# A graph layer on one core: the test of the data moved from ahead of the main loop into it, x loaded in seven pieces, and fewer key columns

## The chip, the cores and the metric

The kernel runs on one NeuronCore of a Trainium2 chip. The metric is device time in microseconds (us) of one execution. Before the change it is 265.71 us, the median of three runs (265.67 to 265.93).

## What is computed

One layer of a graph network over N = 3125 nodes of 128 features and E = 53125 edges, whose list is sorted by destination:

```python
msg = node_feat[src] + edge_feat                                  # (53125, 128)
neigh = jax.ops.segment_sum(msg, dst, num_segments=3125)
rst = (1.0 + eps[0]) * node_feat + neigh
h = rst @ W1 + b1                                                 # 128 -> 256
h = (h - mean) * rsqrt(var + 1e-5) * gamma + beta                 # over the nodes
h = relu(h)
x = layernorm(x + h @ W2 + b2)                                    # over the features
```

## The kernel before

**Groups and windows.** The edges are cut into 208 groups of 256 (two rows of 128 partitions). Since the destinations are sorted, a group touches few neighbouring nodes: a window of 20 columns from the group's first destination. The sum over a group's edge rows is a matmul of the rows with a 0/1 matrix of 20 columns (`edge_sum`, L690), which VectorE makes by a comparison (`hits`, L920). VectorE adds each window into `aggT` at the first destination, which it holds in a register (L1022); registers are loaded 16 at a time (L1012).

**Two ways to node_feat[src].** For 50 groups GpSimd gathers the rows of x by indirect DMA and adds them to the edge rows in `egat` (L438, two gathers a group). For the other 158 the kernel counts: VectorE makes `hit_l` (low 7 bits of the source, L945) and `hit_k` (high part and place in the window, a half A of 25 x 12 = 300 columns, L949, and a half B of 25 x 16 = 400, L952, two groups at once), TensorE multiplies them into a PSUM bank (`counts_a`, L711 and L714, `counts_b`, L720), and ScalarE stores the 500 counts into the fp16 matrix `cnt` (L524). The columns of `cnt` are cut into 9 blocks of nodes, fed by 10, 12, 17, 25, 31, 31, 22, 8 and 2 groups. A block of f is complete when its last group is counted; then it is multiplied with x, in three bf16 parts of 25 tiles, so 75 matmuls (`multiply`, L682), spread over the windows in which the next block is counted. The block widths come out as 114, 180, 256, 376, 468, 466, 332, 120 and 110 columns; blocks begin to be multiplied at w = 13, 30, 52, 83, 122, 163, 192, 204, and the last one after the loop. VectorE adds each product (`add_block`, L986).

**The loop.** `for w in range(G)` runs over the 208 windows; on each engine it is unrolled, and the order is that of the program. A plan by estimated costs (`arrange`) chooses which windows are gathered ones. TensorE may run as far ahead as three PSUM banks of sums and three of counts allow; VectorE's additions lag two windows (LAG), its hits are made ahead (AHEAD, RING_K). In the first nine windows TensorE also turns x (`turn_x`, three tiles a window, L619), ScalarE scales it into `aggT` (L503), and VectorE splits it into parts (`rest`, L971, `part_3`, L979). From the 8th to the 24th counted group two matmuls with no use (L706) go along, to keep TensorE busy. At w = 14 VectorE clears the spare columns of `cnt` (L1039).

**Ahead of the loop.** The lists `dst` and `src` are loaded into 104 partitions (`dstq`, `srcq`), VectorE makes rel (place in the window, L814), hi, lo, key and carry rows (L816 to L828), TensorE turns each into 128 partitions (L582, L600), and engines copy them out of PSUM. VectorE then tests whether the data suit the main path (L837 to L858: windows no wider than 20, groups near their nominal place); TensorE spreads the answer (L605), VectorE stores it in `wide` and signals `path_known` (L872 to L874). All five engines wait for it, load it into a register and branch: the main path, or a general one that assumes nothing.

**Tail.** After the loop: last block, hidden layer in 14 pieces (L636) with its storage on ScalarE (L534) and statistics on VectorE (L1052), moments and scales, relu on both (L541 ScalarE, L1072 and L1074 VectorE), x + b2 (one GpSimd operation, L465) loaded into PSUM by matmuls with the identity (L770), second product (L781), layer norm and output.

**Loads.** SP issues `dst`, then x whole (24 tiles in one DMA, L354, and a last one of 53 rows), then slots and chunks of edges in turn; ScalarE issues `src`, small ones, the first destination of each group (`firsts`), and the weights.

## Time and profile before

| | us |
|---|---|
| median of three runs | 265.71 |
| the profiled execution | 265.49 |
| its span in the profile | 263.7 |
| TensorE (PE) busy | 240.7 (91%) |
| VectorE (DVE) busy | 187.8 (71%) |
| GpSimd (POOL) busy | 172.6 (65%) |
| ScalarE (ACT) busy | 127.9 (48%) |

The busy time of an engine is the time in which one of its instructions runs; PEld is TensorE's loading of weights, which overlaps the matmuls. "Clock" is the TensorE clock that was granted, as a share of 2.4 GHz. The chain of waits starts at the last instruction and goes back, at each step, to what released it or to the instruction before it on its engine. "issue" in it is time in which an engine waited for nothing that the profile shows, and names with a q (DVEq) are the engine's sequencer. A line such as L682 is line 682 of the kernel before.

### The profile page before, as it was taken

Reading aid. Unit: us, or ns where it says so; the run is one execution under the profiler, and the core shown is the slowest. Engines: PE = TensorE matmul, PEld = TensorE weight load, DVE = VectorE, ACT = ScalarE, POOL = GpSimd, SP = SyncE. Lnnn points to the kernel's source line nnn. Section 1 sums busy time; section 2 is a strip of 40 time slices with the busy share of each in tenths; the row PEclk is TensorE's granted clock in tenths of the full one; section 3 lists DMA queues with packets and bytes.
Section 4 is the critical chain, followed back from the end, with each engine's and each line's share of the span. In section 5 each row is a group of like instructions: output and inputs, shape, how many; then the busy total and the mean of one; then the engine's idle time right before and its main releaser. Section 6 shows DMA issues by size and latency. Waiting matters only on the chain.

```text
span 263.7 us, 6841 instructions
## 1 busy us (share of the span) xinstructions
PE 240.7 (91%) x2205; PEld 201.5 (76%) x2205; DVE 187.8 (71%) x686; ACT 127.9 (48%) x225; POOL 172.6 (65%) x113
## 2 busy tenths in 40 slices
PE   0649689999999999999999999999999999999980
PEld 0548568889999998788888888878888879845980
DVE  2978894768789986887887878777666511288882
ACT  0406512445565665455645555544444232176794
POOL 3058888888888888888888888888888600270000
PEclk9999956999999999999999999999999999999996
DMA  5975655677789888777888787877776400000034
GB/s 156 271 232 109 138 115 100 151 153 177 192 193 209 189 196 193 171 184 189 200 186 187 183 193 176 192 165 176 156 160 155 81 0 2 4 0 0 2 114 130
DMA packets 48957, 38.11 MB, mean 145 GB/s; under 512 B 5019, under 2 KB 47947, under 8 KB 48921
## 3 DMA queue, kind: packets, MB, share of 16 engines
q1 hardware_dynamic: 32829, 30.62, 40.3%
q0 software_dynamic: 14400, 6.56, 20.8%
q10 hardware_dynamic: 1692, 0.48, 1.0%
q8 instruction: 19, 0.31, 0.5%
q14 instruction: 17, 0.14, 0.2%
HBM read 36.05 MB, written 1.60 MB: 143 GB/s over the span
## 4 chain that ended last, share of the span: by engine, by line
PE 79%; DVE 12%; issue 3%; ACT 2%; DVEq 2%; DMA 1%; ACTq 1%
PE ps L682 28%; PE ps L690 20%; PE ps L720 9%; PE ps L714 7%; PE ps L636 4%; PE ps L781 3%; PE ps L706 2%; DVE hit_k L952 2%; PE ps L770 2%; DVE hit_k L949 2%; DVE aggT L1022 2%; PE ps L711 1%; ACT big L561 1%; DMA x_room<-in_dst_dram 1%; PE ps L619 1%
## 5 line engine op out<-in xcount | busy, mean ns | idle before, releaser
L438 POOL DMA_INDIRECT egat<-in_x_dram,srci x100 | 163.6, 1636 | 43.1 <-issue 28.3
L524 ACT ACTIVATE big<-ps 128x500 f32 x158 | 96.7, 612 | 109.8 <-PE ps L720 83.6
L690 PEld LDWEIGHTS ps<-hit_c,ebuf 128*128 128x128 f32 x632 | 103.2, 195 | 14.9 <-DVE hit_c L920 4.7
L690 PE MATMUL ps<-hit_c,ebuf 128*128 128x20 f32 x632 | 97.3, 232 | 6.4 <-DVE hit_c L920 4.6
L1022 DVE TENSOR_TENSOR aggT<-aggT,ps 128x20 f32 x208 | 35.9, 173 | 54.9 <-PE ps L690 35.5
L682 PE MATMUL ps<-big,xN 128*128 128x114 f16 (+8 forms) x225 | 59.7, 278 | 0.4 <-ACT big L524 0.3
L682 PE MATMUL ps<-big,x_room 128*128 128x114 f16 (+8 forms) x225 | 59.6, 278 | 0.0
L682 PE MATMUL ps<-big,xr 128*128 128x114 f16 (+8 forms) x225 | 59.5, 278 | 0.0
L720 PE MATMUL ps<-hit_k,hit_l 128*128 128x400 f16 x158 | 53.2, 337 | 0.0
L714 PE MATMUL ps<-hit_k,hit_l 128*128 128x300 f16 x158 | 46.5, 294 | 0.0
L952 DVE TENSOR_TENSOR hit_k<-iota_k,key 128x800 f16<-128x800 f16 x79 | 44.9, 568 | 0.0
L949 DVE TENSOR_TENSOR hit_k<-iota_k,key 128x600 f16<-128x600 f16 x79 | 36.6, 464 | 0.0
L690 PEld LDWEIGHTS ps<-hit_g,egat 128*128 128x128 f32 x200 | 32.7, 195 | 4.9 <-DVE aggT L1022 1.7
L945 DVE TENSOR_TENSOR hit_l<-iota_k,lo 128x512 f16<-128x512 f16 x79 | 33.2, 421 | 1.6 <-issue 1.6
L690 PE MATMUL ps<-hit_g,egat 128*128 128x20 f32 x200 | 30.5, 236 | 1.4 <-DVE aggT L1022 1.4
L682 PEld LDWEIGHTS ps<-big,xN 128*128 128x128 bf16 x225 | 25.0, 111 | 5.7 <-issue 0.9
L711 PE MATMUL ps<-hit_n,hit_l 128*128 128x25 f16 x157 | 29.3, 186 | 0.0
L720 PEld LDWEIGHTS ps<-hit_k,hit_l 128*128 128x128 f16 x158 | 28.5, 180 | 0.0
L711 PEld LDWEIGHTS ps<-hit_n,hit_l 128*128 128x128 f16 x157 | 27.1, 172 | 1.7 <-issue 0.7
L682 PEld LDWEIGHTS ps<-big,x_room 128*128 128x128 bf16 x225 | 24.2, 107 | 4.4
L682 PEld LDWEIGHTS ps<-big,xr 128*128 128x128 bf16 x225 | 24.5, 109 | 3.9
L465 POOL TENSOR_TENSOR xN<-xN,b2e 128x3200 f32<-128x3200 f32 x1 | 7.0, 6960 | 19.5 <-PE ps L682 19.5
(105 smaller groups left out, 209.3 us busy)
## 6 DMA issues: line engine op xcount, KB each, us to landing
ebuf<-in_edge_attr_dram SPq DMA_DIRECT2D x79, 256.0 KB
egat<-in_edge_attr_dram SPq DMA_DIRECT2D x49, 128.0 KB
egat<-in_x_dram,srci POOLq DMA_INDIRECT x100
out_dram<-big SPq DMA_DIRECT2D x5, 256.0 KB
w_sb<-in_L_gnn_W_dram ACTq DMA_DIRECT2D x2, 128.0 KB, 6.9
out_dram<-big SPq DMA_DIRECT2D x2, 128.0 KB
x_room<-in_dst_dram SPq DMA_DIRECT2D x1, 192.0 KB
x_room<-in_src_dram ACTq DMA_DIRECT2D x1, 192.0 KB
```

The costliest lines, as they stand in the source:

```text
L438: return nc.gpsimd.indirect_dma_start(to, None, x[:, :], bass.IndirectOffsetOnAxis(ap=ix, axis=0), compute_op=op)
L524: nc.scalar.activation(cnt[:, :, bass.ds(lows[m % LOADS], WIN)], ps[:, m % BANKS_C, 0:KEYS].rearrange("p (t n) -> p t n", n=WIN), ACT.Copy ...
L636: nc.tensor.matmul(ps[:, n % BANKS_C, 0:width(b)], w1_sb[:, h * P:(h + 1) * P], aggT[:, b * BANK:b * BANK + width(b)], start=True, stop=Tr ...
L682: last = nc.tensor.matmul(ps[:, ACC + f % 2, 0:SIZES[f]], part_v, cnt[:, t, STARTS[f]:STARTS[f] + SIZES[f]], start=(u == 0), stop=(u == UN ...
L690: last = nc.tensor.matmul(ps[:, SUMS + w % BANKS_S, 0:WIN], rows_v[:, j * D:(j + 1) * D], hits_v, start=(j == 0), stop=(j == ROWS - 1))
L711: nc.tensor.matmul(counted(m)[:, :, 0], hit_l[:, (m - 1) % RING_K, 1, :], hit_n[:, (m - 1) // CARRY % 2, (m - 1) % CARRY, :], start=True, ...
L714: nc.tensor.matmul(counted(m)[:, :, 0:WIN_A], hit_l[:, m % RING_K, 0, :], hit_k[:, m % RING_K, 0:KEYS_A].rearrange("p (t n) -> p t n", n=W ...
L720: nc.tensor.matmul(counted(m)[:, :, FROM_B:WIN], hit_l[:, m % RING_K, 1, :], hit_k[:, m % RING_K, KEYS_A:KEYS_A + KEYS_B].rearrange("p (t ...
L945: nc.vector.tensor_tensor(hit_l[:, r:r + 2, :, :].rearrange("p g j (n two) -> p (g j) n two", two=2), pairs(iota_k[:, 0:P]).unsqueeze(1).t ...
L949: nc.vector.tensor_tensor(hit_k[:, r:r + 2, 0:KEYS_A].rearrange("p g (n two) -> p g n two", two=2), pairs(iota_k[:, 0:KEYS_A]).unsqueeze(1 ...
L952: nc.vector.tensor_tensor(hit_k[:, r:r + 2, KEYS_A:KEYS_A + KEYS_B].rearrange("p g (n two) -> p g n two", two=2), pairs(iota_k[:, FROM_B:F ...
L1022: nc.vector.tensor_tensor(to, to, ps[:, SUMS + v % BANKS_S, 0:WIN], ALU.add).then_inc(window_added, 1)
```

## The change

The main path begins without the verdict, on all engines. The first destinations, which address `aggT` and `cnt`, are clamped by two VectorE operations to a range in which every access is within bounds, whatever the data. The tests are in the loop: the reductions in window 85, the rest in window 88 together with the clearing of the spare columns (before in window 14), the matmul that spreads the answer after window 91, its storage and `path_known` in window 94. Each engine branches late: SP after all loads, GpSimd after x + b2, ScalarE and VectorE before the hidden layer's storage and statistics, TensorE after the first four of the preloads of x + b2. If the verdict is bad, the general path loads the lists and x again and does all over.

In the head, key rows are made before lo, PSUM copies of rel, sources and carry go from VectorE to ScalarE, the matmul that shares b2 stands behind four turns, and the row buffers lie in the last columns of `cnt`, since the first ones are now written early. x is loaded in seven pieces, each with a semaphore, between chunks and slots; the weights move from ScalarE's queue to the end of SP's.

Half B of the keys has 15 columns a tile instead of 16 (375 instead of 400; VectorE makes 376 for two to be handled at once), against a list of numbers of its own that starts at 5. MARGIN, the allowed distance from the nominal place, is 30 instead of 36. There are 8 blocks instead of 9; by the same arithmetic their widths are 120, 180, 256, 376, 468, 466, 332 and 218, begun at w = 14, 30, 52, 83, 123, 163, 193 and after the loop. The diff, cut to its core:

```diff
-FROM_B = 4
-WIN_B = WIN - FROM_B
+FROM_B = 5
+WIN_B = 15
-BLOCKS_C = (10, 12, 17, 25, 31, 31, 22, 8, 2)
+BLOCKS_C = (10, 12, 17, 25, 31, 31, 22, 10)
-MARGIN = 36
+MARGIN = 30
+        TEST_F = 3
+        W_BOUNDS = READY[TEST_F] + 2
+        W_TESTS = W_BOUNDS + 3
+        W_WORST = W_TESTS + 3
+        W_SHARED = W_WORST + 3
...
 SP:
-            sp.dma_start(xN[:, 0:NT - 1, :], x_main).then_inc(x_loaded, 16)
-            for n in range(SLOTS):
+            chunk(0)
+            x_piece(X_ORDER[0])
+            slot(0)
+            x_piece(X_ORDER[1])
+            chunk(1)
...
+            for n in range(3, SLOTS):
                 slot(n)
-                if n < CHUNKS:
-                    chunk(n)
+            sp.dma_start(w1_sb[:, :], w1).then_inc(weights_loaded, 16)
...
 GpSimd, ahead of the gathers:
-            pool.wait_ge(path_known, 1)
-            flag = pool.value_load(wide[0:1, 0:1], min_val=0, max_val=1)
+            pool.wait_ge(sources_made, 1)
...
 ScalarE:
+            act.wait_ge(rel_turned, 1)
+            nc.scalar.activation(spread(rel[:, :]), banked(2), ACT.Copy).then_inc(rel_made, 1)
...
+            act.wait_ge(src_turned, 1)
+            nc.scalar.activation(spread(srci[:, :]), banked(7)[:, QC:Q, :], ACT.Copy).then_inc(sources_made, 1)
+            act.wait_ge(carry_turned, 1)
+            nc.scalar.activation(carry[:, :].rearrange("p (q h) -> p q h", h=2),
+                                 ps[:, 1, 0:GC].rearrange("p (h q) -> p q h", q=QC), ACT.Copy).then_inc(carry_made, 1)
...
             act.wait_ge(path_known, 1)
             flag = act.value_load(wide[0:1, 0:1], min_val=0, max_val=1)
+            with act.If(flag == 0):
+                store(hidden_made, hidden_stored)
+            with act.Else():
...
 TensorE:
+                if w == W_WORST:
+                    pe.wait_ge(worst_found, 2)
+                    pe.wait_ge(block_added, TEST_F)
+                    nc.tensor.matmul(ps[:, ACC + (TEST_F + 1) % 2, 0:1], ones[0:Q, :], over[:, TESTS + 1:TESTS + 2],
+                                     start=True, stop=True).then_inc(worst_shared, 1)
...
+            pe.wait_ge(x_b2_added, 1)
+            preload(0, 4)
             pe.wait_ge(path_known, 1)
             flag = pe.value_load(wide[0:1, 0:1], min_val=0, max_val=1)
+            with pe.If(flag == 0):
+                pe.wait_ge(hidden_stored, NB * HH)
+                preload(4, len(ROW_PIECES))
+                products()
+            with pe.Else():
...
 VectorE, ahead of the loop:
+            dve.wait_ge(rel_made, 1)
+            hits_c(0)
             dve.wait_ge(firsts_loaded, 32)
+            dve.wait_ge(constants_made, 10)
+            nc.vector.tensor_tensor(firsts[:, :], firsts[:, :], least_first[:, 0:G], ALU.max).then_inc(lows_made, 1)
+            dve.wait_ge(lows_made, 1)
+            nc.vector.tensor_tensor(firsts[:, :], firsts[:, :], most_first[:, 0:G], ALU.min).then_inc(lows_made, 1)
...
 VectorE, in the loop:
-                    if w == SPREAD * NB:
-                        nc.vector.memset(cnt[:, :, CNT - SPARE:CNT], 0.0).then_inc(spare_zeroed, 1)
+                if w == W_BOUNDS:
+                    find_bounds()
+                if w == W_TESTS:
+                    find_worst()
...
+                    nc.vector.memset(cnt[:, :, CNT - SPARE:CNT], 0.0).then_inc(spare_zeroed, 1)
+                if w == W_SHARED:
+                    dve.wait_ge(worst_shared, 1)
+                    nc.vector.tensor_scalar(wide[:, :], ps[:, ACC + (TEST_F + 1) % 2, 0:1], 0.5, None,
+                                            ALU.is_gt).then_inc(wide_made, 1)
+                    dve.wait_ge(wide_made, 1)
+                    nc.vector.memset(tick[:, 0:1], 0.0).then_inc(path_known, 1)
```

## Rows read from the trace of the kernel before

**Rows 1.** the page: clock and traffic in 40 slices; chain by engine; gathers.

```profile
PEclk9999956999999999999999999999999999999996
...
GB/s 156 271 232 109 138 115 100 151 153 177 192 193 209 189 196 193 171 184 189 200 186 187 183 193 176 192 165 176 156 160 155 81 0 2 4 0 0 2 114 130
...
PE 79%; DVE 12%; issue 3%; ACT 2%; DVEq 2%; DMA 1%; ACTq 1%
...
L438 POOL DMA_INDIRECT egat<-in_x_dram,srci x100 | 163.6, 1636 | 43.1 <-issue 28.3
```

**Rows 2.** chain of waits, head; columns: start us, us, what.

```profile
5.57 0.69 DVE big L814
...
9.17 0.59 DVE most L837
...
11.48 0.15 DVE over L858
11.63 0.50 DVE rel L868
...
12.60 0.89 DVE key L879 x2
...
13.73 0.56 DVEq L886
...
14.71 0.54 issue
...
15.32 0.34 DVE hit_l L945
...
16.90 0.61 PE ps L690 x2
```

**Rows 3.** timeline of the head; columns: start us, us, engine, line, operation.

```profile
6.03 0.76 PE L577 MATMUL ps<-row,ones 1*128 1x129 f32 x2 [6.03 <-DMA row<-in_L_gnn_eps_dram]
...
6.72 1.66 PE L582 MATMUL ps<-ident,big 104*128 104x104 f32 x8
...
15.62 1.69 POOL L438 DMA_INDIRECT egat<-in_x_dram,srci  x1 [12.99 <-DMA egat<-in_edge_attr_dram]
```

**Rows 4.** windows; columns: length, each engine's busy us, clock, DMA share, GB/s.

```profile
29.00:32.00 3.00, 1.57 (x14) 1.15 (x12) 2.15 (x5) 1.68 (x3) 2.39 (x2) 1.00 0.66 116
38.00:44.00 6.00, 6.00 (x37) 4.79 (x36) 3.99 (x13) 1.22 (x2) 5.08 (x4) 0.50 0.49 94
104.00:108.00 4.00, 3.29 (x29) 2.25 (x27) 2.87 (x10) 1.87 (x4) 3.39 (x3) 1.00 0.89 200
108.00:116.00 8.00, 8.00 (x81) 6.88 (x80) 6.97 (x26) 4.58 (x8) 6.78 (x5) 1.00 0.72 164
```

**Rows 5.** chain of waits, middle of the loop.

```profile
87.72 0.09 DVE hit_k L949
...
106.69 0.40 PE ps L690 x2
```

**Rows 6.** groups by line and shape, 30 to 225 us.

```profile
L720 PE MATMUL ps<-hit_k,hit_l 128*128 128x400 f16 x151 | 50.2, 333 | 0.0
L714 PE MATMUL ps<-hit_k,hit_l 128*128 128x300 f16 x151 | 43.9, 290 | 0.0
L952 DVE TENSOR_TENSOR hit_k<-iota_k,key 128x800 f16<-128x800 f16 x73 | 41.5, 568 | 0.0
```

**Rows 7.** chain of waits, last windows and tail.

```profile
221.58 1.00 PE ps L682 x19
...
224.83 3.65 PE ps L682 x75
...
244.82 9.14 PE ps L781 x80
```

**Rows 8.** timeline of VectorE: the clearing; the ready second half of block 0.

```profile
40.62 0.81 DVE L1039 MEMSET big<- 128x900 uint32 x1
...
242.84 0.43 DVE L1074 TENSOR_SCALAR big<-big 128x512 f32<-128x512 f32 x1
```

More of the change, by code:

```diff
@@ L574, in _ @@
             pe.wait_ge(ident_made, 1)
-            pe.wait_ge(row_loaded, 32)
-            pe.wait_ge(constants_made, 2)
-            nc.tensor.matmul(ps[:, 7, 0:D + 1], ones[0:1, :], row[0:1, :], start=True, stop=True).then_inc(b2_shared, 1)
             def turn(bank, v, n):
@@ L621, in turn_x, with hidden @@
                         last.then_inc(x_turned, 1)
+            def hidden(n0, n1, complete, made, stored):
+                for n in range(n0, n1):
+                    b, h = n // HH, n % HH
+                    pe.wait_ge(complete, b + 1)
+                    if n >= BANKS_C:
+                        pe.wait_ge(stored, n - BANKS_C + 1)
+                    nc.tensor.matmul(ps[:, n % BANKS_C, 0:width(b)], w1_sb[:, h * P:(h + 1) * P],
+                                     aggT[:, b * BANK:b * BANK + width(b)], start=True,
+                                     stop=True).then_inc(made, 1)
@@ new lines, in _, with preload @@
+            multiply(F - 1, 0, UNITS)
+            pe.wait_ge(counts_stored, GC)
+            pe.wait_ge(weights_loaded, 80)
+            hidden(0, NB * HH, sums_complete, hidden_made, hidden_stored)
+            def preload(a0, a1):
+                for a in range(a0, a1):
+                    t0, t1 = ROW_PIECES[a]
+                    r = rows_of(t1 - 1)
+                    nc.tensor.matmul(ps[0:r, (a + 4) % 8, 0:(t1 - t0) * D], ident[0:r, 0:r],
+                                     xN[0:r, t0:t1, :].rearrange("p t d -> p (t d)"), start=True, stop=False,
+                                     skip_group_check=True)
@@ L773, in _ @@
[L773 to L783 removed]
+                pe.wait_ge(gen_sums_complete, NB)
@@ L824, in _ @@
                                            in1=rel_h[:, :, P:GROUP], op0=ALU.mult, op1=ALU.add).then_inc(key_rows_made, 1)
+            nc.vector.scalar_tensor_tensor(out=loq, in0=hiq, scalar=float(-P), in1=srcq, op0=ALU.mult,
+                                           op1=ALU.add).then_inc(place_rows_made, 1)
+            dve.wait_ge(key_turned, 1)
+            key_d = key[:, :, :].rearrange("p (q k) two -> p q k two", k=HJ)
+            for a in range(2):
+                last = nc.vector.tensor_copy(key_d[:, :, :, a], banked(3)[:, 0:QC, :])
+            last.then_inc(key_made, 1)
             nc.vector.tensor_tensor(eq_h, dst_h[0:QC, :, P:GROUP], next_h[0:QC, :, :].to_broadcast([QC, 2, P]),
@@ L876, in _ @@
-            dve.wait_ge(key_turned, 1)
-            key_d = key[:, :, :].rearrange("p (q k) two -> p q k two", k=HJ)
-            for a in range(2):
-                last = nc.vector.tensor_copy(key_d[:, :, :, a], banked(3)[:, 0:QC, :])
-            last.then_inc(slots_made, 1)
-            dve.wait_ge(carry_turned, 1)
-            nc.vector.tensor_copy(carry[:, :].rearrange("p (q h) -> p q h", h=2),
-                                  ps[:, 5, 0:GC].rearrange("p (h q) -> p q h", q=QC)).then_inc(slots_made, 1)
```

818 lines of the change are left out of this document (436 added, 382 removed).

## The prediction

> **What bounds the kernel now.** I read the page first, then the chain of waits in order of time, then windows and the timeline where the chain changed engine. TensorE holds 79% of the chain, VectorE 12% [rows 1]. But a share over the whole says little here, because there are three kinds of stretch.
>
> The head: up to 16.90 us TensorE has no window to work on. The chain is VectorE's alone [rows 2]: from the landing of the destination list (5.57) through place and key rows, the minima and maxima, the tests (to 11.63), the copies out of PSUM, the load of the verdict (13.73) and the jump behind it, to the first key hits at 15.32. Then, to about w=12, VectorE remains the later engine: TensorE waits on its additions, and TensorE's clock is granted at 0.50 (the 1.2 GHz level) for about 10 us around 38 to 44 [rows 1, 4].
>
> The loop from there: the chain lies on TensorE, except 87.72 to 106.69, where it is VectorE's without a break [rows 5]. By the code's plan block 2 ends before w=83 and is added at w=84; in the chain that addition comes some three microseconds before the stretch ends, so the stretch ends at about w=86.
>
> The tail, from 224.83: last block, hidden layer, preloads, second product, all on TensorE [rows 7].
>
> **The head, step by step.** VectorE's work between 9.17 and 12.60 is mostly tests and copies. What goes: minimum, maximum and tests, 9.17 to 11.63 = 2.46 us; the copies of rel and srci and the verdict, 11.63 to 12.60 = 0.97, less 0.05 for the padding that stays; the copy of carry, 0.24 (from 12.60 + 0.89 to 13.73); verdict load and jump, 13.73 to 15.32 = 1.59. Sum 5.22 us [rows 2]. What comes: two operations on the 208 first rows, not in the trace; bounds 0.3 (two small tests at 0.15 each, the 11.48 row) and 1.2 (two of 0.59, the reduction of 512 elements at 9.17); I take 0.6, nearer the small ones since one partition of 208 elements is under half of 512, plus two waits. And two waits on TensorE's turns. From the list's landing at 5.57, a 0.69 and four operations of about 0.4 make the key rows, which no longer wait for lo: ready near 7.4. Turning rel and key takes 4 transposes each, half of the 8 in 1.66 us [rows 3], so key is turned at about 8.3, where VectorE arrives at 8.0: 0.3 us. The shared bias now stands behind four turns (rel, key, lo, src, to 9.9 us) and takes 0.76 [rows 3]; VectorE, at 10.0 with carry, waits for it until about 10.6: 0.6. ScalarE takes over the copies; it has 5 fewer DMAs to issue before them, and its copy of lo ends near 10, srci and carry near 11, before VectorE asks. So VectorE gains 5.2 - 0.6 - 0.9 = 3.7; less 0.2 for waits not counted, **3.5 us** (2.5 to 4.5). The first key hits then start at about 11.9, and TensorE's first counts about 13.2. Since to w=12 VectorE is the later engine and its work there is otherwise unchanged, the whole shift is kept. GpSimd moves too: its first gather stood behind the verdict, at 15.62 [rows 3], and may start near 10.5. Its 100 gathers take 1.64 us and 0.30 of issue each [rows 1], 194 us in all: before, done near 210 where the last window ends at 224.8; now near 205 against some 218. It stays some 13 us ahead.
>
> **Seven pieces of x.** Costed at nothing: chunk 0 and x piece 0 are first on SP's queue, 0.5 MB; behind them the pieces alternate with chunks and slots. If traffic moves as before (156 GB/s in the first 6.6 us, 0.4 MB of it lists, then 271 [rows 1]), the first two are there near 6.5 us, piece 4 near 8, chunk 1 near 9, the last piece of x near 16; that one is turned from w=8 (over 20 us) and split from w=7. The cover is thick for x, thinner for the first rows (`firsts`), which VectorE now needs near 11.3 instead of 13.73 [rows 2]: the trace shows only that they had landed by then. Bounds 0 and 2.4 us; I take 0, since nothing waited. The weights, moved behind the slots on SP, are used 200 us later.
>
> **Keys of 375 columns.** Counts of half B: the 400-column matmul is 333 ns, the 300-column one 290 [rows 6], 0.43 ns a column, so 25 columns are 10.8 ns. Of 158 groups some 137 lie where TensorE is on the chain: 1.5 us. In VectorE's stretches its own hits shrink from 800 to 752 elements, 6% of 568 ns = 34 ns per pair of groups [rows 6], some 10 pairs, 0.3. Together **1.8 us** (0 if the odd stride of 15 costs what the columns save; 2.1 if all groups count). The 34 filler matmuls lose 25 columns too: 21 ns at half clock, 10 at full, **0.4 us**.
>
> **Blocks.** Sizes from the code: the last three were 332, 120, 110 columns, now 332 and 218. In the loop 75 matmuls of 120 columns go: 19 take 1.00 us, so 3.95 us; at the end 75 of 110 took 3.65 [rows 7], and 218 columns at 2.4 GHz are 91 ns plus the 3 ns seen at 110 (48.7 against 45.8), 7.05 us: 3.4 more. Net **0.55 us** gained; bounds 0 and 1.
>
> **The tests in the loop.** Now at w=85 (minimum, maximum: 2 of 0.59 = 1.18 [rows 2]), w=88 (the rest of the 2.46, 1.28, and the clearing of the spare columns, 0.81 [rows 8], which before lay at w=14, while TensorE was busy throughout [rows 4]), w=94 (0.2): together 3.5 us on VectorE. They come at the very end of the stretch in which VectorE was last (to 106.69 [rows 5]), and from 108 to 116 it is busy 6.97 of 8 us [rows 4]. Queued behind them are its own additions and key hits; TensorE may run only some two windows ahead of the additions. The slack in ten windows is about 1 us. So **2.4 us** of it is paid (bounds 0.8, if the ring of hits covers each piece, and 3.5, if none is covered). TensorE's one-column product lies where it waits anyway; bounds 0 and 0.76, the first row of [rows 3], and I put 0.1. The verdict is out near w=96, its first wait is at w=123: no wait.
>
> **The tail.** Each engine now branches there. GpSimd, SyncE: off the chain. ScalarE and VectorE jump over the general path between last statistics and moments; a jump was followed by 0.54 us without work [rows 2]. Block 0 of the second relu half was ready at 242.84 + 0.43 = 243.27 [rows 8], TensorE came to it at 244.82 [rows 7]: 1.5 us of cover, so 0; without it 0.54. TensorE loads the verdict between its preloads. VectorE's whole load and jump was 1.59 us [rows 2]. Before TensorE's stand four preloads of 512 columns, over 2 us on the array, so if its sequencer works ahead of the array it is hidden. Bounds 0 and 1.6; I take 0.2 for both. The Trainium skill, "Runtime: NRT & Kernel Launch", section "Instruction fetch mechanics", says that a taken branch to a page not held forces a fetch before work goes on; no row shows such a fetch apart from the 0.54 us; by that row nothing is added behind the 1.5 us of cover, by a longer fetch only what exceeds it. "TensorE: Matmul & The Clock Gate" (its table of specifications) gives TensorE a queue of 64, by which the second branch would be hidden whole.
>
> **Sum.** -3.5 -1.8 -0.4 -0.55 +2.4 +0.1 +0.2 = -3.55 us. The profiled execution took 265.49 us (span 263.7, 1.8 around it); less 3.55 is 261.9, and against the median of the runs, 265.71, **262.2 us**.
>
> **The rivals.**
> A: the stretch at half clock is shorter or falls away, since all before it moves. It came after TensorE had been starved near 30 us (busy 1.57 of 3). From 38 to 44 TensorE was busy 6.00 of 6 at half, 3.0 of work at 2.4 GHz; VectorE wanted 3.99 less the clearing's 0.81 [rows 4, 8], with its gaps about 3.5. So 2.5 us would go there and 0.4 beside it: 259.3. For it: filler matmuls meet an earlier start. Against: the starving itself is unchanged.
> B, the slower one: the tests starve TensorE near w=85 to 95 as the head did near 30 us, and the clock falls there. Price: 3.5 instead of 2.4, and 10 us at half as in [rows 1], up to 5 us lost, less 1 where VectorE leads: 262.2 + 1 + 4 = 267.2. It decides if TensorE starves there as it did between 29 and 32 us, before the clock fell. Against: 104 to 108 had 3.29 of 4 busy without a fall [rows 4].
> C: the tests are hidden (0.8 paid): 260.6.
> D: the head is bound by transfers, and starting sooner only waits for `firsts` or chunks: the 3.5 are gone, 265.7. Against: nothing in the trace waits on those loads, which are now first in the queue.
>
> **Chances.** Forecast 0.62 (own range 260.3 to 264.3), A 0.14, C 0.08, D 0.07, B 0.09. A difference of 0.2% (0.53 us) is about what can be told from none: faster 0.84, same 0.07, slower 0.09. The range takes in A's and D's times, each widened by what the bounds of head and tests add: 258.5 to 266.2; B is left out, with little else.
>
> **What would show it.** Key hits starting at 11 to 12.5 us (head); counts matmuls of half B near 322 ns (keys); 75 final matmuls in about 7 us; TensorE waits on VectorE's additions of about 2.4 us near w=85 to 95; hidden layer to second product as long as before. Wrong if counts start after 14 us, if granted clock 0.50 appears after 100 us, or if the half-clock stretch changes by over 4 us.

## The result, and the profile after

The changed kernel took 269.62 us, the median of four runs (267.22 to 271.2), against 265.69 for the kernel before (265.31 to 265.93): 1.0142 times as long, 95% interval 1.0084 to 1.0199. The prediction was 262.2 with a range of 258.5 to 266.2, and faster at 0.84. It was slower. Twelve more runs later gave 267.18 (265.16 to 271.17), ratio 1.0048, interval 1.0015 to 1.0080; the sixteen together have a median of 268.0. So the sign stands, and the size is 1.5 to 4 us. The intervals leave out executions more than 1.5% above the fastest of their kernel (four of these twelve, six of the ten in e10), which is why there the ratio doesn't match the medians. The experiments ran on three chips; the median of the kernel before was 265.62 to 266.15 us beside them, and each ratio is against the executions on the same chip.

The page of the changed kernel's profiled execution (271.2 us, the longest of the sixteen; span 269.3), which stands against [rows 1]: TensorE's busy time; the granted clock in 40 slices; the shares of the chain.

```profile
PE 248.5 (92%) x2130; PEld 207.6 (77%) x2130; DVE 185.8 (69%) x684; ACT 128.6 (48%) x228; POOL 176.5 (66%) x116
...
PEclk9999958999999999579999999999999999999996
...
PE 80%; DVE 10%; issue 2%; ACT 2%; DMA 2%; DVEq 2%; ACTq 1%
```

TensorE's share of the chain rose from 79 to 80% and VectorE's fell from 12 to 10%, and the kernel still got longer. The clock row says where to look. Its first fall, at slices 6 and 7, is that of [rows 1]. The second, at slices 17 and 18 (108 to 121 us), is new.

The head, from the timeline (start us, length us, engine, line, operation; in brackets what ended the idle time before it), against [rows 2, 3]:

```profile
6.86 0.69 DVE L930 TENSOR_TENSOR big<-big 104x512 f32<-104x512 int32 x1 [4.99 <-DMA big<-in_dst_dram]
...
9.73 0.91 DVE L944 CAST key<-ps 128x316 f16<-128x316 f32 x2 [0.45 <-PE ps L661]
...
11.84 0.29 DVE L952 COPY b2e<-ps 128x129 f32<-128x129 f32 x1 [0.45 <-PE ps L679]
...
12.38 1.76 POOL L510 DMA_INDIRECT egat<-in_x_dram,srci  x1 [8.80 <-ACT srci L569]
12.49 0.36 DVE L1062 TENSOR_TENSOR firsts<-firsts,big 1x208 int32<-1x208 int32 x1
...
13.25 0.41 DVE L1014 TENSOR_TENSOR hit_l<-iota_k,lo 128x512 f16<-128x512 f16 x1
...
14.55 0.43 PE L769 MATMUL ps<-hit_k,hit_l 128*128 128x300 f16 x1 [1.02 <-DVE hit_k L1021]
```

The first key hits start at 13.25 us; before they started at 15.32. That is 2.1 us earlier, not the 3.4 of the forecast. The first row shows why: the destination list lands at 6.86, before at 5.57. From the landing to the first key hits it is 6.39 us, and 9.75 before, a gain of 3.4 us, so the working from one to the other was right. The two clamps are 0.36 each (I had 0.3 for one), and each wait on TensorE's turns 0.45 (I had 0.3 and 0.6). GpSimd's first gather starts at 12.38, where 10.5 was forecast; nothing waits for it.

The middle, from the chain in order of time, against [rows 5]:

```profile
101.60 0.41 DVE aggT L1055
...
102.05 1.10 DVEq L1082
...
103.36 0.18 DVE aggT L1100
...
103.79 0.46 DVE hit_k L1018
104.25 0.46 DVE hit_k L1021
104.72 0.28 DVE hit_n L1032
104.99 0.60 DVE most L959
105.59 0.59 DVE least L960
...
106.32 0.40 PE ps L739 x2
```

At w = 85 everything comes together: the addition of block 2 (L1055), the loading of 16 registers (L1082, 1.10), key hits (L1018, L1021), carry hits (L1032), and now the two reductions. Between the window additions at 103.36 and at 106.18 there is none, and TensorE, which may run only some two windows ahead, mostly stands still. The windows of that stretch (busy us of PE, PEld, DVE, ACT and POOL with instruction counts, then granted clock, DMA share, GB/s), against [rows 4]:

```profile
104.00:106.00 2.00, 0.46 (x4) 0.21 (x3) 2.00 (x5) 0.15 (x1) 1.70 (x2) 1.00 0.87 196
106.00:108.00 2.00, 1.68 (x16) 1.42 (x17) 1.57 (x7) 0.60 (x1) 1.70 (x2) 0.97 0.46 80
108.00:110.00 2.00, 2.00 (x11) 1.56 (x10) 1.59 (x14) 0.65 (x1) 1.70 (x2) 0.50 0.85 163
...
116.00:118.00 2.00, 2.00 (x12) 1.66 (x13) 1.05 (x4) 0.63 (x2) 1.54 (x1) 0.50 0.75 164
118.00:120.00 2.00, 2.00 (x20) 1.72 (x20) 1.16 (x5) 0.98 (x2) 1.73 (x1) 0.97 0.46 82
```

From 104 to 106 us TensorE is busy 0.46 of 2. Then its clock is granted at 0.50, the 1.2 GHz level, for 10 us: 11 matmuls run from 108 to 110 us, where 20 do from 118 to 120 (the counts in brackets). This is rival B, which had 0.09.

The end, from the longest pieces of the chain, against [rows 7]:

```profile
226.69 7.01 PE ps L731 x75
...
244.43 5.57 PE ps L833 x16
250.00 9.14 PE ps L847 x80
```

The last 75 matmuls take 7.01 us (forecast 7.05). From the start of the second product to the end it is 19.3 us, 18.9 before: 0.4 more, where 0.2 was forecast for the branches. That the branches cause it was not tried.

### The profile page after: what moved, and what is told of

Read it like the earlier page. It is cut to its first block, busy times and chain, and to the rows that moved or that the text cites. A ratio compares the mean times of both kernels' runs of the same rounds, so it can differ in the third digit from the quotient of the medians.

```text
span 269.3 us, 6711 instructions
## 1 busy us (share of the span) xinstructions
PE 248.5 (92%) x2130; PEld 207.6 (77%) x2130; DVE 185.8 (69%) x684; ACT 128.6 (48%) x228; POOL 176.5 (66%) x116
## 4 chain that ended last, share of the span: by engine, by line
PE 80%; DVE 10%; issue 2%; ACT 2%; DMA 2%; DVEq 2%; ACTq 1%
PE ps L731 28%; PE ps L739 20%; PE ps L775 10%; PE ps L769 7%; PE ps L711 4%; PE ps L847 3%; PE ps L761 2%; PE ps L833 2%; DVE hit_k L1021 2%; DMA big<-in_dst_dram 2%; PE ps L766 2%; DVE hit_k L1018 1%; ACT big L643 1%; DVE xr L1040 1%; DVE aggT L1100 1%
## 5 line engine op out<-in xcount | busy, mean ns | idle before, releaser
L510 POOL DMA_INDIRECT egat<-in_x_dram,srci x100 | 166.5, 1665 | 40.3 <-issue 28.0
L739 PEld LDWEIGHTS ps<-hit_c,ebuf 128*128 128x128 f32 x632 | 107.6, 202 | 12.1 <-DVE aggT L1100 4.0
L739 PE MATMUL ps<-hit_c,ebuf 128*128 128x20 f32 x632 | 99.5, 236 | 3.2 <-DVE aggT L1100 2.5
L731 PE MATMUL ps<-big,xr 128*128 128x120 f16 (+7 forms) x200 | 59.3, 298 | 0.0
L731 PE MATMUL ps<-big,x_room 128*128 128x120 f16 (+7 forms) x200 | 59.3, 298 | 0.0
L731 PE MATMUL ps<-big,xN 128*128 128x120 f16 (+7 forms) x200 | 59.2, 298 | 0.1
L775 PE MATMUL ps<-hit_k,hit_l 128*128 128x375 f16 x158 | 56.2, 356 | 0.0
L1021 DVE TENSOR_TENSOR hit_k<-iota_b,key 128x752 f16<-128x752 f16 x79 | 42.8, 542 | 0.0
L1018 DVE TENSOR_TENSOR hit_k<-iota_k,key 128x600 f16<-128x600 f16 x79 | 36.6, 463 | 0.0
L731 PEld LDWEIGHTS ps<-big,xN 128*128 128x128 bf16 x200 | 22.5, 112 | 5.3 <-issue 0.4
L731 PEld LDWEIGHTS ps<-big,xr 128*128 128x128 bf16 x200 | 22.6, 113 | 4.4 <-issue 0.5
```

The source lines that it names most:

```text
L510: return nc.gpsimd.indirect_dma_start(to, None, x[:, :], bass.IndirectOffsetOnAxis(ap=ix, axis=0), compute_op=op)
L731: last = nc.tensor.matmul(ps[:, ACC + f % 2, 0:SIZES[f]], part_v, cnt[:, t, STARTS[f]:STARTS[f] + SIZES[f]], start=(u == 0), stop=(u == UN ...
L739: last = nc.tensor.matmul(ps[:, SUMS + w % BANKS_S, 0:WIN], rows_v[:, j * D:(j + 1) * D], hits_v, start=(j == 0), stop=(j == ROWS - 1))
L775: nc.tensor.matmul(counted(m)[:, :, FROM_B:WIN], hit_l[:, m % RING_K, 1, :], hit_k[:, m % RING_K, KEYS_A:KEYS_A + KEYS_B].rearrange("p (t ...
L1018: nc.vector.tensor_tensor(hit_k[:, r:r + 2, 0:KEYS_A].rearrange("p g (n two) -> p g n two", two=2), pairs(iota_k[:, 0:KEYS_A]).unsqueeze(1 ...
L1021: nc.vector.tensor_tensor(hit_k[:, r:r + 2, KEYS_A:KEYS_A + KEYS_E].rearrange("p g (n two) -> p g n two", two=2), pairs(iota_b[:, :]).unsq ...
```

## Where the time lies, kernel by kernel

The same milestones were read from the timeline and chain of every kernel: the start of the addition of block 0 (the end of the head), of block 2 and of block 3 (the tests lie between), and of the last 75 matmuls.

| kernel | block 0 | 2 | 3 | 2 to 3 | last 75 | block 0 to last 75 |
|---|---|---|---|---|---|---|
| before | 59.04 | 103.06 | 137.51 | 34.45 | 224.83 | 165.79 |
| changed | 57.28 | 101.60 | 143.18 | 41.58 | 226.69 | 169.41 |
| changed, again (e14) | 58.24 | 102.57 | 140.75 | 38.18 | 224.23 | 165.99 |
| no tests (e2) | 57.06 | 101.40 | 136.89 | 35.49 | 220.36 | 163.30 |
| tests spread (e13) | 58.09 | 102.42 | 139.25 | 36.83 | 222.70 | 164.61 |
| before + tests' work (e3) | 59.99 | 103.82 | 140.61 | 36.79 | 227.93 | 167.94 |
| before + 375 keys (e4) | 59.08 | 103.31 | 137.86 | 34.55 | 225.81 | 166.73 |
| before + 350 keys (e9) | 58.15 | 101.28 | 135.06 | 33.78 | 221.20 | 163.05 |
| no tests, 350 keys (e7) | 53.58 | 96.90 | 131.59 | 34.69 | 213.25 | 159.67 |

One profile a kernel, so differences under a microsecond are not to be trusted: the changed kernel and e14 are the same program, and block 0 differs by 0.96. But the column "2 to 3" says what the tests cost in the loop: against the kernel without them 1.3 us spread, 2.7 with the clock at half for some 3.4 us, 6.1 with it at half for 10 us.

## Experiments

**e1: the tests earlier.** The same tests in windows 32 to 41, one block edge after the first.

```diff
-        TEST_F = 3
+        TEST_F = 1
```

> The changed kernel with its tests in the stretch of block 1 (windows 32 to 41) instead of block 3 (85 to 94); nothing else. Theory S (starving): in the profile of the changed kernel the additions of blocks 2 and 3 are 41.6 us apart against 34.4 before, VectorE's tests leave TensorE busy only 0.46 of 2 us near 105, and the clock then stands at 0.50 from 108 to 118. So the tests' place costs some 7 us, and here, where VectorE was busy 1.2 to 2.2 of 3 us, most of it returns: 262 to 264. Rival K (the keys or blocks): the loss lies in the odd stride of 15 columns or in the new blocks and not in the tests: 268 to 270.

Measured: 269.49 us (267.88 to 271.82, 4 runs), ratio 1.0183 (1.0105 to 1.0261). Theory S missed. The time is what rival K named, but the trace shows that this place is no better: TensorE starves there too (busy 2.44 of 4 us from 60 to 64 us), the granted clock is 0.77 and 0.80 in the two windows of 4 us behind it, and block 0 to block 1 takes 23.2 us instead of the 19.2 of the changed kernel.

**e2: no tests.** All minima, maxima and comparisons left out; the verdict is set to good by a constant; the clearing stays at w = 88.

```diff
-                nc.vector.tensor_reduce(most[:, :], rel_t, AX_X, ALU.max)...
-                nc.vector.tensor_reduce(least[:, :], rel_t, AX_X, ALU.min)...
...
+                nc.vector.memset(over[:, TESTS + 1:TESTS + 2], 0.0).then_inc(worst_found, 2)
```

> The changed kernel without the tests' work: the minima, maxima and comparisons are left out, the verdict is set to good by one clearing of a column; the clearing of the spare columns stays in window 88, and so do all waits and branches. Theory S: no fall of the clock after 100 us, 261 to 263, at most 1.5 us from the kernel with early tests. Rival K: 268 to 270. Rival L (the clearing alone is enough to bring the clock down): 266 to 269, with a stretch at 0.50 after 105 us.

Measured: 265.01 us (263.57 to 267.45, 10 runs), ratio 0.9984 (0.9943 to 1.0025), between what theory S and rival K named; no half clock after 100 us. Windows of its trace, as above:

```profile
104.00:106.00 2.00, 1.32 (x13) 0.94 (x13) 1.57 (x8) 0.08 (x1) 1.70 (x2) 1.00 0.94 218
106.00:108.00 2.00, 2.00 (x20) 1.50 (x19) 1.86 (x6) 1.42 (x3) 1.69 (x2) 1.00 0.57 138
```

Two things follow. The tests cost the changed kernel 2.2 us in the medians (267.18, on another chip) and 4.6 against its first four runs. And without any test the rest of the change gains 0.4 us by the ratio and 1.1 by the medians, where the forecast had 6.05 (3.55 + 2.4 + 0.1): most of the miss has nothing to do with the tests.

**e3: the kernel before, with the tests' work added in the loop.** Same sizes of VectorE operations at w = 85 and 88, on other data and with no use for the result; the clearing moved from w = 14 to 88. The tests ahead of the loop stay.

```diff
+                    if w == READY[3] + 2:
+                        nc.vector.tensor_reduce(most[:, :], again, AX_X, ALU.max)...
+                        nc.vector.tensor_reduce(least[:, :], again, AX_X, ALU.min)...
+                    if w == READY[3] + 5:
+                        for k in range(10): nc.vector.tensor_scalar(over[:, 2*k:2*k+2], spot, ...)
+                        ...
-                    if w == SPREAD * NB:
                         nc.vector.memset(cnt[:, :, CNT - SPARE:CNT], 0.0)
```

> The kernel before, its head untouched, with VectorE work of the size of the tests added in windows 85 (two reductions of 104 x 512 values) and 88 (twelve small operations), and the clearing of the spare columns moved from window 14 to 88. Theory S: the clock falls after 100 us here too, and the time grows by 5 to 8 us to 271 to 274. Rival K: the tests' work is worth at most its own 3.3 us, below 269.

Measured: 269.2 us (268.3 to 269.77, 4 runs), ratio 1.0146 (1.0082 to 1.021). Theory S missed: the profile has no half clock after 100 us, although TensorE is busy only 1.00 of 2 us from 106 to 108. The interval from block 2 to 3 is 2.3 us longer, which is the forecast's 2.4. The time is 3.05 us longer than the 266.15 measured beside it; about 0.95 of that lies ahead of block 0 in the profile, before the added work. So the work's own price was sized rightly here, and it lengthens the kernel without any fall of the clock; in e13 the same work, spread, costs 1.3, so the 2.3 is no fixed price.

**e4: the kernel before, with 375 keys** and the margin of 30.

```diff
-FROM_B = 4
-WIN_B = WIN - FROM_B
+FROM_B = 5
+WIN_B = 15
-MARGIN = 36
+MARGIN = 30
```

> The kernel before with 375 columns of keys in half B, and with the allowed distance from the nominal place at 30 instead of 36, which makes room for the second list of numbers (block widths 120, 180, 256, 376, 468, 466, 332, 120 and 98). Theory S: this part gives about what was forecast, 1.8 us and 0.4 for the fillers: 263.2 to 264.2. Rival K: 266 or more.

Measured: 266.44 us (264.3 to 267.56, 10 runs), ratio 1.0032 (0.9996 to 1.0069). Missed: no gain at all, although the margin alone shortens the last block from 110 to 98 columns (its 75 matmuls 3.26 us instead of 3.65). Groups of matmuls from 120 to 175 us, where the clock is at 2.4 GHz (line, engine, output and inputs, shape, count, busy us, mean ns of one), first e4, then e5:

```profile
L724 PE MATMUL ps<-hit_k,hit_l 128*128 128x375 f16 x48 | 16.3, 339 | 0.0
...
L686 PE MATMUL ps<-big,x_room 128*128 128x468 f16 x25 | 9.1, 363 | 0.0
```

```profile
L720 PE MATMUL ps<-hit_k,hit_l 128*128 128x400 f16 x49 | 16.1, 329 | 0.0
L714 PE MATMUL ps<-hit_k,hit_l 128*128 128x300 f16 x49 | 14.1, 288 | 0.0
...
L682 PE MATMUL ps<-big,x_room 128*128 128x468 f16 x25 | 9.0, 359 | 0.0
```

**e5: the margin of 30 alone** on the kernel before.

```diff
-MARGIN = 36
+MARGIN = 30
```

> The kernel before with the allowed distance at 30 instead of 36 and nothing else: the row of cnt is 2416 instead of 2422 columns long and the blocks begin at 120, 300, 556, 932 instead of 114, 294, 550, 926. Theory P (pitch): in the keys kernel and in the one without tests the block matmuls of 468 columns took 362 ns against 359 and those of 376 columns 324 against 321, though their widths are unchanged; if the new pitch of cnt does that, it is 362 and 324 here too, and with some 600 such matmuls the time grows by about 0.5 to 1.5 us. Rival: it came with the keys: 359 and 321 here, time unchanged within 0.3 us.

Measured: 266.0 us (265.17 to 269.88, 10 runs), ratio 1.0026 (0.9988 to 1.0065): no difference that can be told. The 375-column count takes 339 ns, the 400-column one 329: fewer columns take longer. The block matmuls, unchanged, take 3 to 4 ns more (363 against 359) in the kernel with 375 keys and not in the one with the margin alone, so that comes with the keys as well.

**e6: 375 keys from an even column.** The kernel without tests, half B at columns 4 to 18; the last column of each window is left out of the counts, so the output lacks those edges, and two more filler matmuls go along in each of the first three groups. One run.

```diff
-FROM_B = 5
+FROM_B = 4
-                nc.tensor.matmul(counted(m)[:, :, FROM_B:WIN], ...
+                nc.tensor.matmul(counted(m)[:, :, FROM_B:FROM_B + WIN_B], ...
```

> The changed kernel without the tests' work, half B written to columns 4 to 18 of each tile instead of 5 to 19 (15 columns still, an even start), so edges in column 19 are left out of the counts; two more fillers in each of the first three groups set the column that is then never written, and the fillers' weights are 0/1 values. The 375-column matmul of half B took 339 ns against 329 for 400 columns and 318 expected. If the odd start costs it, about 318 here; if the odd number of columns does, about 328; if the stride of 15 in the moving data does, 339.

```profile
L779 PE MATMUL ps<-hit_k,hit_l 128*128 128x375 f16 x49 | 16.2, 330 | 0.0
```

At full clock 300 columns take 288 ns and 400 take 329 (e5), 0.41 ns a column, which makes 319 for 375. e4 lies 20 ns above that line and e6, at 330, 11: 9 ns go with the odd start, 11 stay with the odd width of 15: none of the three values expected. The keys are read in the same way in both kernels, so the start can only matter on the output's side, in the PSUM bank; for the width this was not separated. The one run took 264.71 us, which is e2's time within what a single run tells.

**e7: 350 keys**, half B at columns 6 to 19, 14 wide, on the kernel without tests. The main path then suits fewer lists: in half B no edge may lie ahead of column 6 of its window. One run.

```diff
-FROM_B = 5
-WIN_B = 15
+FROM_B = 6
+WIN_B = 14
```

> The changed kernel without the tests' work, with half B on columns 6 to 19 (14 a tile, 350 in all), so edges of half B in column 5 are left out of the counts. By the slope of 0.43 ns a column below the 329 ns of 400 columns it is 308 ns; if a cost of some 20 ns comes with the odd start and number only, it is 308; if it comes with any other stride than 16, 328.

Measured: 257.81 us (the kernel before beside it 265.62), and 308 ns a count, as expected and on the line (288 + 50 x 0.41), and the block matmuls are back at 359. It is 7.2 us less than e2. In the table 3.6 of these lie between block 0 and the last 75 (some 140 counts x 31 ns = 4.3, less where VectorE sets the pace), and 3.5 in the head, which is another matter (below).

**e8: tests in the first block, 400 keys**, on the changed kernel (windows 16 to 25; the wait of the one-column product on the block's addition goes, since no block is added yet).

```diff
-        TEST_F = 3
+        TEST_F = 0
-FROM_B = 5
-WIN_B = 15
+FROM_B = 4
+WIN_B = 16
```

> The changed kernel with the tests in windows 16 to 25, where TensorE ran at half clock and VectorE was busy 0.18 of 3 us (41 to 44 us), and with 400 columns of keys again. Theory S: the tests cost under 1 us there and the clock stands at 1.00 from 45 us on: against the kernel without tests (265.0) the keys give back about 1: 263.5 to 265. Rival: TensorE is starved by any 3 us of VectorE work in the loop wherever it stands: 267 to 269.

Measured: 264.46 us (263.33 to 265.46, 10 runs), ratio 0.9982 (0.9952 to 1.0012). As expected. Better than the changed kernel by 2.7 in the medians, 1.8 by the ratios, and no fall of the clock after 45 us; but the edit changes place and keys at once, and what each gives was not separated.

**e9: the kernel before with 350 keys.** The edit of e4 with 6 and 14.

> The kernel before with half B of the keys at columns 6 to 19 instead of 4 to 19: 14 columns, 350 keys (and the margin of 30); nothing else. Theory W (the price of a count matmul follows its columns as long as the width per tile is even; the 15 columns of the changed kernel fall off that line): 308 ns instead of 329 for the second half, 158 windows x 21 ns = 3.3 us, so 262 to 262.8. Rival (the counts' matmuls end earlier but TensorE then waits for the key hits of VectorE, as long as before): 265 to 266.

```profile
L724 PE MATMUL ps<-hit_k,hit_l 128*128 128x350 f16 x49 | 15.1, 308 | 0.0
...
L686 PE MATMUL ps<-big,x_room 128*128 128x468 f16 x25 | 9.0, 358 | 0.0
```

Measured: 261.93 us (261.19 to 264.42, 10 runs), ratio 0.9893 (0.9852 to 0.9934). Theory W holds: 21 ns less a count, 3.9 us less in all, 0.4 of it from the shorter last block that comes with the margin. Two columns a tile taken away instead of one give more than the 2.2 us that I had booked for one.

**e10: the changed kernel with 350 keys**, the edit of e7, tests at w = 85.

> The changed kernel with 350 keys instead of 375, tests at their place in window 85. Theory W: 31 ns less in each of 158 counts (339 to 308) and 3 ns less in the four block matmuls of a window, 4.9 + 1.9 = 6.8 us: 262 to 263.5. If the width of 15 is only dear in some positions, and the 7 us between the two kernels without tests came from other places of the half clock: 265 to 268.

Measured: 266.21 us, ratio 0.9895 (0.9848 to 0.9942). The ten runs lie in two groups: four from 261.81 to 264.68, six from 266.11 to 267.71. The profiled one (267.38) is of the upper group:

```profile
104.00:108.00 4.00, 2.62 (x26) 2.29 (x27) 3.47 (x18) 1.25 (x2) 3.28 (x3) 1.00 0.68 100
108.00:112.00 4.00, 2.59 (x22) 2.15 (x20) 3.29 (x17) 1.18 (x2) 3.39 (x3) 0.90 0.63 135
112.00:116.00 4.00, 4.00 (x24) 3.39 (x25) 3.10 (x13) 1.18 (x2) 3.39 (x3) 0.50 0.73 138
```

TensorE is busy 2.62 and 2.59 of 4 us while the tests run, and then the clock is at 0.50. The lower group is about where theory W put it (262 to 263.5). The mean granted clock on record is 0.978 to 0.980 in all six of the upper group, as in the traced one, and 0.958 or 0.987 in the lower four. That the lower group is without the fall is not shown: none of the four has a trace, and the kernel before, which has no tests in the loop, splits too (beside e1 fifteen executions up to 266.55 us and four from 267.72 to 269.55).

**e11: tests in the first block and 350 keys** (the edits of e8 and e7).

> The changed kernel with 350 keys and the tests in windows 16 to 25 (first block). With 400 keys and the tests there it took 264.5; 21 ns x 158 = 3.3 us less gives 261.1, and the same difference as between the kernels without tests (375 to 350: 7 us) would give 258 to 259. Above 262: the tests there cost more once TensorE needs less time per window.

Measured: 262.18 us (260.75 to 263.01, 6 runs), ratio 0.986 (0.9816 to 0.9904): 2.3 less than e8 (3.2 by the ratios, the two ran on different chips), where 3.3 was expected. No fall of the clock after the head, and no second group in six runs.

**e12: the dst list ahead of the large loads**, on the changed kernel.

```diff
+            sp.wait_ge(dst_loaded, 80)
             chunk(0)
             x_piece(X_ORDER[0])
```

> The changed kernel (375 keys, tests in window 85), with SyncE waiting for the dst list to land before it issues the first chunk of edges and the first piece of x. Theory H (the list lands 1.3 us later than before because these loads share the DMA engines with it): the list is there at 5.6 us instead of 6.9, the first key hits 1.3 us earlier, and the time 1.0 to 1.3 us shorter, 268.3. Rival (what then comes late is the first chunk and x, issued 3.4 us later, and the first windows wait for those): 269.5 to 271. If the list lands at 6.9 all the same, the loads were not the cause.

Timeline of its head:

```profile
5.81 0.69 DVE L931 TENSOR_TENSOR big<-big 104x512 f32<-104x512 int32 x1 [3.95 <-DMA big<-in_dst_dram]
...
12.19 0.41 DVE L1015 TENSOR_TENSOR hit_l<-iota_k,lo 128x512 f16<-128x512 f16 x1
```

The list is there at 5.81 instead of 6.86, and the first key hits start at 12.19 instead of 13.25: the loads issued behind the list were what held it up. The size varies: the ten traced kernels with the changed kernel's loads have the list at 6.20 (e14) to 7.35 us, the three that wait for it at 5.54 to 5.81. I had costed the seven pieces of x at nothing by asking whether they would be there in time, and not what they would do to the 0.2 MB that stand ahead of them. The time, 266.44 us (265.53 to 270.35, 10 runs), ratio 1.0037 (0.9993 to 1.0081), is 0.7 below the changed kernel's twelve runs, within what the two measurements can tell. The profile, which has the clock at 0.54 and 0.61 from 108 to 112 us, says why so little came of it: see the next section.

**e13: the tests spread.** One reduction in window 86, one in 88, the comparisons in 89 to 92, the clearing in 94, the one-column product in 95.

```diff
-                if w == W_BOUNDS:
-                    find_bounds()
-                if w == W_TESTS:
-                    find_worst()
+                if w == W_BOUNDS + 1:
+                    find_bounds(False)
+                if w == W_BOUNDS + 3:
+                    find_bounds(True)
+                if W_TESTS <= w <= W_TESTS + 3:
+                    find_worst(w - W_TESTS)
```

> The changed kernel with the same tests cut into single steps: one reduction in window 86, one in 88, the comparisons in 89 to 92, the clearing in 94, the one-column product in 95. VectorE does the same work, but never more than some 0.7 us of it between two windows. If the starving of TensorE and the fall of the clock behind it are the larger part (rival B): no half clock after 100 us, and the time near that without tests plus what is left of the work, 265 to 266.5. If the tests' work itself costs it, wherever it stands: 269 to 270, as the changed kernel.

**e14: the changed kernel once more**, unedited, on the same chip.

> The changed kernel once more, unedited, beside the spread one. If the fall of the clock is the larger part, its times lie in two groups, one near 267 without the fall and one near 270 to 271 with it. If the tests' work is all of it, the times lie together near 269.6.

Measured: e13 266.58 us (264.41 to 268.65, 12 runs), ratio 1.0031 (0.9991 to 1.0071); e14 267.18, as above. Windows of e13, then of e14:

```profile
104.00:106.00 2.00, 1.32 (x10) 0.74 (x8) 1.80 (x7) 0.71 (x2) 1.70 (x2) 1.00 0.71 167
106.00:108.00 2.00, 2.00 (x20) 1.73 (x21) 1.80 (x6) 0.71 (x2) 1.70 (x2) 1.00 0.60 123
...
110.00:112.00 2.00, 1.43 (x14) 1.07 (x13) 1.81 (x15) 0.45 (x1) 1.70 (x2) 1.00 0.75 182
112.00:114.00 2.00, 2.00 (x21) 1.70 (x19) 1.86 (x7) 1.18 (x3) 1.70 (x2) 1.00 0.84 183
```

```profile
104.00:106.00 2.00, 1.42 (x10) 0.71 (x7) 1.67 (x6) 0.79 (x2) 1.70 (x2) 1.00 0.78 166
106.00:108.00 2.00, 0.72 (x8) 0.65 (x9) 1.57 (x6) 0.00 (x0) 1.70 (x2) 1.00 0.47 98
108.00:110.00 2.00, 2.00 (x14) 1.60 (x13) 1.90 (x14) 0.97 (x2) 1.70 (x2) 0.61 0.69 149
110.00:112.00 2.00, 2.00 (x13) 1.35 (x12) 1.68 (x10) 0.87 (x2) 1.70 (x2) 0.54 0.41 59
112.00:114.00 2.00, 2.00 (x23) 1.86 (x23) 1.60 (x8) 0.59 (x1) 1.70 (x2) 1.00 0.76 176
```

Spread, TensorE never falls under 1.32 of 2 us and keeps its full clock; in one piece it is busy 0.72 of 2 and the clock falls for some 3 us. All four traced executions with the tests in one piece at w = 85 (the changed kernel, e10, e12, e14) show such a fall. How much starving it takes these traces don't tell: e3, busy 3.88 us of the 6 from 106 to 112, kept its clock, and e10, busy 5.21 of 8, lost it.

The twelve times of e14 lie eight from 265.16 to 268.6 and four from 269.53 to 271.17, less cleanly apart than I had expected. The mean granted clock, on record for each execution, tells a little more. Of the changed kernel's sixteen, five have 0.984 or 0.985, as e14's traced one with its fall, and take 268.6 to 270.06 us; three have 0.992 or 0.993, as e13's traced one without, and take 266.21 to 267.22. So the fall seems not to be in every execution; it is an inference, since two of the sixteen have a trace. Spreading is worth 0.6 us in the medians and 1.45 in the means (266.53 against 267.98), which is twice the standard error of 0.7. What it leaves is the work: e13 is 1.6 above e2 in the median, 1.25 by the ratios.

**e15: 350 keys, tests in the first block, dst list first** (e11 + e12).

> 350 keys, tests in windows 16 to 25, and SyncE waiting for the dst list before its first chunk. With 350 keys and the tests there it took 262.2; the list 1.05 us earlier should give 261.1. If TensorE leaves half speed in the head earlier as well, as in the 257.8 kernel: 258 to 259.

**e16: 350 keys, tests spread, dst list first** (e13 + e7 + e12).

> 350 keys, the dst list first, and the tests spread over windows 86 to 95. From the changed kernel: keys -6, list -1.05, no fall of the clock -3.5, which gives 259 to 260 from 269.6. If the tests' own work is the larger part: 262 to 263.

Measured: e15 259.84 us (259.35 to 260.8, 6 runs), ratio 0.9808 (0.9765 to 0.9851); e16 260.36 (257.44 to 262.76, 6 runs), ratio 0.9786 (0.9716 to 0.9857). Both beat both kernels, by 2% or so; e15's runs lie closer together. e15 lies between its two expected values, e16's median just above its first. e15 is 2.3 below e11, 1.4 by the ratios. The earlier list is the only edit between them, but in e11's trace TensorE is at half speed without a break until 43.10 us and in e15's it isn't, so how much the list gives by itself stays open.

## The head: TensorE at half speed where the granted clock says 1.00

The 300-column count matmul is a gauge of TensorE's speed. In the changed kernel's timeline:

```profile
24.64 0.43 PE L769 MATMUL ps<-hit_k,hit_l 128*128 128x300 f16 x1
...
27.88 0.29 PE L769 MATMUL ps<-hit_k,hit_l 128*128 128x300 f16 x1
...
34.19 0.43 PE L769 MATMUL ps<-hit_k,hit_l 128*128 128x300 f16 x1
...
43.44 0.29 PE L769 MATMUL ps<-hit_k,hit_l 128*128 128x300 f16 x1
```

0.43 us up to 24.64, 0.29 from 27.88, 0.43 again from 34.19 to 41.57, 0.29 from 43.44. Only the second slow stretch shows as a granted clock of 0.50; in the first the windows say 1.00 and the matmuls take as long as at 0.50. The Trainium skill, "TensorE: Matmul & The Clock Gate", Part 1, says that half rate is the state from which the engine starts, and that activity lifts it; it also warns that the recorded clock events are not reliable. The trace agrees with the start at half rate and with the warning. It does not bear out the rise by activity as simply as that: in e12 TensorE is busy 27.76 of the 28 us from 14 to 42 and still at 0.43 at 42.47. In the kernel before the first slow stretch ends between 23.35 and 24.50 and the second lies from 35.10 to 41.85.

The end of this half speed, more than the start of the key hits, sets where the head ends. In e12, e13 and e14 the matmul is at 0.43 without a break until about 42 us; from e12:

```profile
42.47 0.43 PE L770 MATMUL ps<-hit_k,hit_l 128*128 128x300 f16 x1
...
44.05 0.29 PE L770 MATMUL ps<-hit_k,hit_l 128*128 128x300 f16 x1
```

Block 0 is added at 57.90, 58.09 and 58.24, later than in the changed kernel (57.28), although their key hits start at 12.19, 12.87 and 12.59 instead of 13.25. In the traces of all kernels but e16, block 0 is added 13.2 to 15.7 us after the first 300-column matmul that is back at 0.29 for good, whether the key hits started at 11.9 or at 15.6. In e7 TensorE is at full speed from 20.26, slow again by 28.43 and fast from 37.87 on: block 0 at 53.58. In e16 it stays fast from here on:

```profile
29.62 0.42 PE L770 MATMUL ps<-hit_k,hit_l 128*128 128x300 f16 x1
...
31.28 0.29 PE L770 MATMUL ps<-hit_k,hit_l 128*128 128x300 f16 x1
```

and block 0 is added at 52.71, 5.4 us earlier than in e13 with the same work but for the keys and the list. So a head of nearly the same code differs by some 5 us with when TensorE comes up to speed. What decides that in one kernel and not in the next I can't say; no run was made for it alone.

## Why the prediction was wrong

By the terms of its sum:

- **Keys, -1.8 and -0.4: wrong.** e4 gives +0.85 by its ratio (-0.1 to 1.8), so 2.2 to 3 us of the miss, the margin's possible share included. The step that failed is "25 columns are 10.8 ns": the slope between two even widths was applied to an odd one. I had written the case down as a bound ("0 if the odd stride of 15 costs what the columns save") and then taken the other end, with no row for it. It wasn't even the end: 339 against 329 lies beyond it.
- **Head, -3.5: mis-sized, and one step wrong.** The first key hits came 2.1 earlier (2.7 in e14), block 0's addition 1.8 (0.8 in e14). The operations were right to 0.15 us; missing was the later landing of the list, 1.3 us (0.6 in e14), which e12 traced to the loads behind it. The step that failed besides is "the whole shift is kept", since VectorE was to stay the later engine up to w=12. From 14 to 42 us TensorE is busy 22.29 of 28 before and 27.77 in e14, nearly all of it at half speed, and its waits on VectorE's additions there shrink from 2.5 us to 0.2: what comes earlier runs into TensorE itself.
- **Tests in the loop, +2.4: right for the work** (2.3 in e3; 1.3 when spread), but in the changed kernel a fall of the clock came on top, 3.8 us in the profiled execution (6.1 against 2.3) and 0.4 to 1.4 in e14's (2.7 against 2.3 or 1.3).
- **Rival B, 0.09: too small.** It was priced at 267.2 and decided by "if TensorE starves there as it did between 29 and 32 us", and it did: 0.46 of 2. What I held against it, that 104 to 108 had 3.29 of 4 busy, was the kernel before without the tests in that place. The two reductions of 1.2 us, behind a register load and three hit operations in the same window, had to be laid over those rows and weren't. Moreover the range left B out whole.
- **Blocks, -0.55: near its lower bound of 0,** as far as one profile each can tell: 7.01 at the end against 7.05; in the loop e2 and e4, which share the 375 keys and the margin, differ by 3.43 us between block 0 and the last 75, against 3.95. That leaves a gain of 0.1 (3.43 less the 3.36 by which 7.01 exceeds 3.65).
- **Tail, +0.2:** 0.4 to 0.8 in all kernels with the late branch, cause not tried. The four preloads ahead of TensorE's load, put at "over 2 us", take some 1.4 us by the 16 in 5.57 above. **One-column product, +0.1:** TensorE waits there for nothing that the chain shows.

Added up from the profiles of the kernel before and of e2, whose profiled executions differ by 0.5 us where 6.05 was forecast without the tests: the head 1.5 short (3.5 against 2.0), the keys 3.1 (0.94 lost in e4 between block 0 and the last 75, 2.2 forecast), the blocks 0.5, the tail 0.5. Together 5.6, where 5.55 is to be explained; the sum has to agree, since the terms divide one difference, but how they divide it rests on one profile a kernel. The tests are no part of the miss in the twelve runs: 2.2 us against the 2.5 forecast. In the first four runs they cost 4.6, so there 2.1 us more of the miss are theirs.

## What to carry to other kernels

Before a matmul's width is cut, look whether the new width and start per tile are even: here runs of 14 cost 21 ns less than runs of 16, and runs of 15 from an odd column 10 ns more. Work moved into a loop that has slack on average should be cut to the size of the slack between two steps and kept away from windows in which loads of registers and other batches fall; the sum of busy time in ten windows says nothing on whether the other engine starves for two microseconds, and for TensorE that can be followed by microseconds at half its clock. A load that is wanted first should be finished, not only issued first, before megabytes are put behind it: that brought the list 0.4 to 1.8 us forward, though in e12 nothing that can be told from noise in the time. And before an earlier start is booked as gained, look at what the engine that takes over does with it: here TensorE was at half speed until some 43 us and used the gain up.

## What was not expected of the hardware

- A count matmul with fp16 inputs and 375 columns in 25 runs of 15 takes 339 ns from an odd start column and 330 from an even one; 400 in runs of 16 take 329, 350 in runs of 14 take 308.
- With the 375 columns the block matmuls between them, themselves unchanged, take 3 to 4 ns more; with an even start 2 to 3.
- In the first 20 to 45 us matmuls run at half speed (0.43 us for 0.29), in part where the granted clock reads 1.00, and when that ends differs by over 10 us between kernels that differ in little (31.28 in e16, 44.05 in e12).
- Chunks and pieces of 128 to 256 KB, issued behind a list of 0.2 MB, delay its landing: 6.20 to 7.35 us in ten traces, 5.54 to 5.81 in the three in which they wait for it.
